# A graph attention layer that streams a 256 MB adjacency matrix: TensorE turns two chunks of the next strip before its maxima, the target rows are computed two pieces later, the index work of narrow strips moves forward, and x is read back into unused parts of the ring

## The reference, cut to what matters

```python
h = jnp.maximum(_layernorm(x, axis=-1), 0.0)                    # x: [8192, 128]
proj = jnp.einsum('nf,hfo->hno', h, W)                          # 4 heads
scores = jax.nn.leaky_relu(s_src[:, :, None] + s_tgt[:, None, :], negative_slope=0.2)
attn = jax.nn.softmax(mask[None, :, :] + scores, axis=1)        # mask: adj, [8192, 8192], values up to 1e9
vals = jnp.einsum('hij,hjo->hio', attn, proj)
vals = jax.nn.elu(vals + h[None, :, :])
out = x + vals.mean(axis=0)
```

## Time and profile before

| what | value |
|---|---|
| median of 3 runs | 993.73 us (992.29 to 1092.76) |
| the profiled execution | 993.13 us, span 991.4 us |
| busy share of the span | DVE 81%, PE 74%, ACT 69%, POOL 24% |
| mean DMA rate over the span | 297 GB/s (290.27 MB by SP's queue, 4.20 MB by POOL's) |
| exponentials, L498 | 512 of 1086 ns, and 512 readings of the sum of 196 ns |
| chunks turned, L440 | 4096 transposes |
| maxima of wide pieces, L557 and L561 | 3.12 us each on the mean |

### The profile page before, as it was taken

The page is one execution under the profiler, slowest core; times in us unless marked ns, Lnnn a source line. Parts: engine busy times, 40 slices in busy tenths (PEclk is TensorE's granted clock), DMA queues, the critical chain, the costliest instruction groups (busy, mean ns, idle before and its releaser), DMA issues.

```text
span 991.4 us, 14968 instructions
## 1 busy us (share of the span) xinstructions
PE 734.1 (74%) x4995; PEld 609.6 (61%) x4995; DVE 807.4 (81%) x812; ACT 684.3 (69%) x1173; POOL 234.7 (24%) x164
## 2 busy tenths in 40 slices
PE   0419597797797797797797797797797798609882
PEld 0317477777777677677677677687687686504330
DVE  3976888888888888888888888888888877327996
ACT  0598496696696696696786786786786788544542
POOL 1000211221221221221212212212212202215885
PEclk9759798898898898898898898998998999859997
DMA  9999999999999999999999999999999976076111
GB/s 245 337 382 384 372 370 337 370 331 325 369 330 323 370 328 325 369 327 323 372 325 321 373 324 325 373 326 324 375 323 324 364 234 173 9 207 150 53 54 55
DMA packets 224068, 294.93 MB, mean 297 GB/s; under 512 B 4512, under 2 KB 218016, under 8 KB 224032
## 3 DMA queue, kind: packets, MB, share of 16 engines
q1 hardware_dynamic: 214816, 290.27, 85.7%
q0 software_dynamic: 9216, 4.20, 3.5%
HBM read 281.80 MB, written 12.65 MB: 297 GB/s over the span
## 4 chain that ended last, share of the span: by engine, by line
PE 33%; DVE 28%; issue 11%; ACT 10%; DMA 8%; POOL 6%; SPq 2%; ACTq 0%; POOLq 0%; DVEq 0%
PE ps L440 23%; DVE arena L561 19%; ACT ps L498 9%; PE ps L405 7%; DMA arena<-in_adj 6%; POOL arena L391 4%; DVE arena L570 3%; SPq L332 2%; DVE arena L578 2%; POOL arena L395 2%; DMA sums<-arena 2%; PE ps L424 1%; DVE arena L623 1%; ACT arena L519 1%; PE ps L412 1%
## 5 line engine op out<-in xcount | busy, mean ns | idle before, releaser
L498 ACT ACTIVATE ps<-ps,arena 128x1024 f32<-128x1024 f32 x512 | 556.0, 1086 | 225.6 <-PE ps L440 198.8
L440 PE MATMUL ps<-ident,arena 128*128 128x128 f32 x4096 | 572.3, 289 | 52.1 <-ACT ps L498 50.1
L440 PEld LDWEIGHTS ps<-ident,arena 128*128 128x128 f32 x4096 | 480.1, 149 | 130.3 <-ACT ps L498 126.3
L561 DVE TENSOR_TENSOR arena<-arena 128x3072 f32<-128x3072 f32 (+2 forms) x115 | 359.3, 3125 | 13.6 <-DMA arena<-in_adj 10.3
L378 POOL DMA_INDIRECT sums<-arena x64 | 157.0, 2453 | 641.4 <-DVE arena L617 313.6
L405 PE MATMUL ps<-ident,arena 128*128 128x128 f32 x512 | 93.2, 342 | 152.6 <-DVE arena L570 151.1
L405 PEld LDWEIGHTS ps<-ident,arena 128*128 128x128 f32 x512 | 80.7, 183 | 157.9 <-issue 89.0
L578 DVE TENSOR_REDUCE arena<-ps 128x1 f32<-128x1024 f32 x64 | 78.3, 1224 | 54.2 <-PE ps L405 54.2
L498 ACT ACTIVATION_READ_ACCUMULATOR ps<-ps,arena 128x1 f32 x512 | 100.2, 196 | 0.0
L557 DVE TENSOR_TENSOR arena<-arena 128x3072 f32<-128x3072 f32 (+2 forms) x23 | 71.8, 3122 | 16.4 <-DMA arena<-in_adj 16.4
L583 DVE SCALAR_TENSOR_TENSOR ps<-ps,arena 128x1024 f32<-128x1024 f32 x64 | 82.1, 1283 | 0.3 <-issue 0.3
(11 more groups left out here) (74 smaller groups left out, 195.8 us busy)
## 6 DMA issues: line engine op xcount, KB each, us to landing
arena<-in_adj SPq DMA_DIRECT2D x160, 1536.0 KB, 13.7
arena<-in_adj SPq DMA_DIRECT2D x16, 512.0 KB, 7.2
arena<-in_adj SPq DMA_DIRECT2D x8, 1024.0 KB, 11.0
sums<-arena SPq DMA_DIRECT2D x1, 4160.0 KB, 22.4
arena<-sums SPq DMA_DIRECT2D x8, 512.0 KB, 7.3
out<-arena SPq DMA_DIRECT2D x16, 256.0 KB, 2.3
sums<-arena POOLq DMA_INDIRECT x64, 7.2
w_sb<-in_L_gnn_W SPq DMA_DIRECT2D x1, 256.0 KB, 2.7
```

The costliest lines, as they stand in the source:

```text
L440: mm = pe.transpose(turned_ps[n % 2][:, m, :], piece(i, r, nq)[:, m, q * P:(q + 1) * P], ident[:, :])
L498: act.activation(turned_ps[n % 2], turned_ps[n % 2], ACT.Exp, scale=KAPPA, bias=cert[:, i, q, G:G + 1], accum_out=cert[:, i, q, r:r + 1]). ...
L561: dve.tensor_tensor(acc_of(nq), acc_of(nq), piece(i, r, nq), ALU.max).then_inc(f_acc, 1)
```

## The change

It does five things.

1. PE turns chunks c0 and c1 of a strip before that strip's `turn_maxima` of sub-strip 0: at the end of the strip before it, behind that strip's last chunk (`EARLY = 2`; for strip 0 before the strips begin). Inside a strip `turn_maxima` of sub-strip 1 then follows that of sub-strip 0 directly.
2. DVE computes the target rows after the fifth `piece_max` of the next strip (piece 5), no longer after the third (piece 3).
3. In the strip of 256 columns `turn_idx`, `sum_same` and `copy_sum` stand after chunks 5, 8 and 9 (before: 8, 13, 15), in the last strip of 128 columns after chunks 2, 3 and 4 (before: 5, 7, 7). For wide strips they stay at 8, 13 and 15.
4. x is read into parts of slots 8 to 11 that the last, narrow strip doesn't use (16 row tiles in each), in four DMAs that SP issues directly behind the last piece of adj, without the wait for all chunks.
5. The tail's buffers `e` and `s2` are separate tiles in the front of these four slots. Their sizes and the instructions on them are the same.

```diff
+    LAST_SLOT = 8
+    XT = NT // (RING - LAST_SLOT)
...
-    x_rows = D.take([NT, O])
...
-    e = D.take([2, 2, H, O])
     m = D.take([4, 2, H, O])
-    s2 = D.take([4, 2, 2, O])
     s1 = D.take([4, 2, O])
+    e, s2, x_rows = [], [], []
+    for b in range(RING - LAST_SLOT):
+        X = Arena(c["arena"], S0 + (LAST_SLOT + b) * RT * WIDE)
+        if b < 2:
+            e.append(X.take([2, H, O]))
+        else:
+            s2 += [X.take([2, 2, O]), X.take([2, 2, O])]
+        x_rows.append(X.take([XT, O]))
...
-    IDX_AT, SUM_AT, COPY_AT = 8, 13, 15
+    IDX_AT = {1: 2, 2: 5, 3: 8}
+    SUM_AT = {1: 3, 2: 8, 3: 13}
+    COPY_AT = {1: 4, 2: 9, 3: 15}
+    EARLY = 2
...
-            sp.wait_ge(f_turn, NT * G)
-            for k in range(2):
-                tiles = slice(k * NT // 2, (k + 1) * NT // 2)
-                sp.dma_start(x_rows[:, tiles, :], x_t[:, tiles, :]).then_inc(t_x, 16)
+            for k in range(RING - LAST_SLOT):
+                sp.dma_start(x_rows[k], x_t[:, k * XT:(k + 1) * XT, :]).then_inc(t_x, 16)
...
+            def turn_chunk(g, i, n):
+                nq = subs(g, i)
+                r, q = order(nq)[n]
+                pe.wait_ge(f_exp, at(g, i, n) + 1)
+                if q == 0:
+                    pe.wait_ge(f_in[slot(i, r)], landed(g, i, r))
+                for m in range(RT):
+                    mm = pe.transpose(turned_ps[n % 2][:, m, :], piece(i, r, nq)[:, m, q * P:(q + 1) * P], ident[:, :])
+                mm.then_inc(f_turn, 1)
+
             def strip(g, i):
...
                 turn_maxima(g, i, 0)
-                for n, (r, q) in enumerate(chunks):
+                for n in range(EARLY, nq * G):
                     if n % LEAD == LEAD - 1 and n // LEAD + 1 < nq:
                         turn_maxima(g, i, n // LEAD + 1)
...
+                    turn_chunk(g, i, n)
                     if not first_strip(g, i):
-                        if n == min(IDX_AT, nq * G - 3):
+                        if n == IDX_AT[nq]:
                             turn_idx(*former_of(g, i))
-                        if n == min(SUM_AT, nq * G - 1):
+                        if n == SUM_AT[nq]:
                             sum_same(*former_of(g, i))
+                if not last_strip(g, i):
+                    for n in range(EARLY):
+                        turn_chunk(*latter_of(g, i), n)
...
-                    if not first_strip(g, i) and n == min(COPY_AT, nq * G - 1):
+                    if not first_strip(g, i) and n == COPY_AT[nq]:
                         copy_sum(*former_of(g, i))
...
                     piece_max(*after, 3)
+                    piece_max(*after, 4)
+                    piece_max(*after, 5)
                 if not first_strip(g, i):
                     find_target(*before)
                 if not last_strip(g, i):
-                    piece_max(*after, 4)
-                    piece_max(*after, 5)
                     piece_max(*after, 6)
```

More of the change, by code:

```diff
@@ L167, in peaked_path @@
     stage = D.take([2, QUAD * P])
-    e = D.take([2, 2, H, O])
     m = D.take([4, 2, H, O])
-    s2 = D.take([4, 2, 2, O])
     s1 = D.take([4, 2, O])
-    assert D.at <= S0 + RING * RT * WIDE
+    assert D.at <= S0 + LAST_SLOT * RT * WIDE
+    e, s2, x_rows = [], [], []
[6 more added lines that the diff above has]
+        x_rows.append(X.take([XT, O]))
+        assert X.at <= S0 + (LAST_SLOT + b + 1) * RT * WIDE
     turned_ps = [c["psum"][b][:, :].rearrange("p (t i) -> p t i", i=P) for b in range(2)]
@@ L390, in _ @@
                     pool.wait_ge(t_s1, w - 3)
-                pool.tensor_tensor(s2[:, w % 4], m[:, w % 4, :, 0:2, :], m[:, w % 4, :, 2:4, :], ALU.add).then_inc(t_s2, 1)
+                pool.tensor_tensor(s2[w % 4], m[:, w % 4, :, 0:2, :], m[:, w % 4, :, 2:4, :], ALU.add).then_inc(t_s2, 1)
                 pool.wait_ge(t_s2, w + 1)
@@ L394, in _ @@
                     pool.wait_ge(t_o, w - 3)
-                pool.tensor_tensor(s1[:, w % 4], s2[:, w % 4, :, 0, :], s2[:, w % 4, :, 1, :], ALU.add).then_inc(t_s1, 1)
+                pool.tensor_tensor(s1[:, w % 4], s2[w % 4][:, :, 0, :], s2[w % 4][:, :, 1, :], ALU.add).then_inc(t_s1, 1)
         @block.tensor
@@ L427, in sum_same @@
                 mm.then_inc(f_sum, 1)
+            def turn_chunk(g, i, n):
[7 more added lines that the diff above has]
+                mm.then_inc(f_turn, 1)
             def strip(g, i):
-                nq, Q = subs(g, i), number(g, i)
-                chunks = order(nq)
+                nq = subs(g, i)
                 turn_maxima(g, i, 0)
-                for n, (r, q) in enumerate(chunks):
+                for n in range(EARLY, nq * G):
                     if n % LEAD == LEAD - 1 and n // LEAD + 1 < nq:
                         turn_maxima(g, i, n // LEAD + 1)
[L436 to L441, removed]
+                    turn_chunk(g, i, n)
                     if not first_strip(g, i):
-                        if n == min(IDX_AT, nq * G - 3):
+                        if n == IDX_AT[nq]:
                             turn_idx(*former_of(g, i))
-                        if n == min(SUM_AT, nq * G - 1):
+                        if n == SUM_AT[nq]:
                             sum_same(*former_of(g, i))
+                if not last_strip(g, i):
+                    for n in range(EARLY):
+                        turn_chunk(*latter_of(g, i), n)
             def turn_sums(k):
@@ L467, in _ @@
             pe.wait_ge(s_ident, 1)
+            for n in range(EARLY):
+                turn_chunk(0, 0, n)
             strips_of(pe, strip)
@@ L543, in _ @@
                     act.wait_ge(t_m, w - 1)
-                act.activation(e[:, w % 2], v_ps[w % 3], ACT.Exp, scale=1.0 / PART, bias=e_bias).then_inc(t_e, 1)
+                act.activation(e[w % 2], v_ps[w % 3], ACT.Exp, scale=1.0 / PART, bias=e_bias).then_inc(t_e, 1)
                 k = w * 2 // QUAD + 2
@@ L691, in elu @@
                     dve.wait_ge(t_s2, w - 3)
-                dve.scalar_tensor_tensor(m[:, w % 4], e[:, w % 2], PART, v_ps[w % 3],
+                dve.scalar_tensor_tensor(m[:, w % 4], e[w % 2], PART, v_ps[w % 3],
                                          ALU.min, ALU.max).then_inc(t_m, 1)
@@ L697, in finish @@
                 dve.wait_ge(t_s1, w + 1)
-                dve.scalar_tensor_tensor(osb[:, tiles, :], s1[:, w % 4], -1.0, x_rows[:, tiles, :],
+                dve.scalar_tensor_tensor(osb[:, tiles, :], s1[:, w % 4], -1.0, x_rows[2 * w // XT][:, 2 * w % XT:2 * w % XT + 2, :],
                                          ALU.add, ALU.add).then_inc(t_o, 1)
@@ L741, in _ @@
             assert count[0] == CHECKS
-            dve.wait_ge(t_x, 32)
+            dve.wait_ge(t_x, 16 * (RING - LAST_SLOT))
             for w in range(PAIRS + 4):
```

## The result

| | before | changed |
|---|---|---|
| median | 993.68 us | 937.42 us (935.8 to 938.15) |
| profiled span | 991.4 us | 934.1 us |
| mean granted clock of TensorE | 0.89 | 0.93 |

The ratio is 0.9436, 95% interval 0.9417 to 0.9455. The forecast was 943 in a range of 921 to 966. One of the four executions of the kernel before took 1092.76 us, and the ratio is taken without it.

What follows compares the result with a forecast made beforehand. No engine was full: a ring of waits bound each strip through three loops (DVE, ACT with PE, DMA). Middle strips 39.2 us, then -0.9, 4.2 and 7.8 at the end, gave 50.3 off 993.13: 943 us, range 921 to 966.

Steps and rivals of the forecast that it cites:

- DVE's and PE's loops: Rings of waits in wide strips: DVE's at 34.4 us, ACT and PE's at 34.5, so a 34.5 us period, clock up.
- fallen strips: Wide strips where PE's clock falls: 35.7 us each, expected in two of three, for a mean period of 35.3.
- the hole: PE idle 3.0 us between a strip's first and second turns of maxima, where its clock can fall, costing 1.2 us.
- Strip 20: First strip after the 18 middle periods, 34.38 us before: 0.9 us lost to the clock's risk.
- strip 21: Next-to-last strip, 29.55 us before: PE bounds it at 24.8, saving 4.8, less 0.6 for the clock: 4.2.
- M(22) to the last landing: From strip 22's first turn of maxima to the last add's landing: 7.8 us saved, 2.8 by an earlier first add.
- chunks c0 and c1 ahead: In wide strips PE turns them while idle, nothing added; DVE's last reduction starts 9.4 us into the strip, not 10.8.
- `find_target` two pieces later: In DVE's loop in wide strips: its stop of 1.7 us goes and nothing takes its place, with 5 us to spare.
- A: Rival: PE's clock holds, all middle strips take 34.5 us, 66.1 us less, 927 us; chance 0.25.
- B: Rival: PE's clock falls in each strip and stays down past c3, 36.6 us a strip, 969 us; chance 0.13.
- E: Rival: the DMA queue is full, the period stays at 37.5 us, only the end's 11 us are gained, 982; chance 0.08.
- D: Rival, slower: one more low clock stretch a strip on PE loses 2.6 us, period 39.2, 1016 us; chance 0.04.

Runs made afterwards that it cites:

- E3: The changed kernel with 16 transposes of the identity, whose result nobody reads, between each strip's first and second turn of maxima: 927.67 us, ratio 0.9337.
- E7: The changed kernel with x read, to its new place, only after all chunks are turned: 941.23 us, ratio 0.949.
- E8: The changed kernel with the narrow strips' index work put back at its old places: 941.16 us, ratio 0.9485.
- E1: The kernel before with one edit, `find_target` moved behind the next strip's fifth `piece_max`: 936.42 us, ratio 0.9434.
- E2: The changed kernel with only the two chunks ahead left; `find_target`, narrow strips' index work and x's read time put back: 1001.36 us, ratio 1.0071.
- E6: The changed kernel with no chunk turned ahead (`EARLY = 0`): 926.60 us, ratio 0.9336.
- E4: The changed kernel with one chunk turned ahead, not two (`EARLY = 1`): 930.08 us, ratio 0.9369.
- E11: The changed kernel without look-ahead, with half of each piece not read from strip 3 on, same instructions: 925.3 us, ratio 0.9304.
- E5: The kernel before with 16 transposes of the identity, whose result nobody reads, behind each strip's last chunk: 972.16 us, ratio 0.9796.

## Why the prediction was right, and where it was not

**Right, with the sum near.** 50.3 us were forecast, 56.3 came. In the strips the forecast had 39.2 us, and 45.3 came: DVE's and PE's loops at 34.5 were 34.2 to 34.3, the second turn of maxima stood at M+4.0 (forecast 4.1), fallen strips took 35.2 to 36.0 (35.7), but the clock fell in 7 of 18 and not in 12. At M = 605.01 DVE was ready about 0.2 us before PE, so the loops did meet. That the clock falls over the hole was a mechanism taken from two rows, and E3 confirmed it. The Trainium skill (TensorE: Matmul & The Clock Gate, section on HAM oscillation) would have had it stay up over a gap of this length; here it fell over an idle gap of 2.93 us in 7 middle strips, and the measurement decides. One reading of the rows was off without a term resting on it: the DMA engines stood still for under three microseconds in the strip at M = 377.92 (a share of 0.46 at 389 to 390, 0.02 at 390 to 392, 0.91 at 392 to 393), not for four.

**The end, nearly right with two errors that cancel.** Strip 20 lost nothing (forecast 0.9), strip 21 gained 3.6 (4.2; its 25.95 us lie above the 24.8 to 25.4 that were to be the sign), and M(22) to the last landing gained 7.7 (7.8). In that last term I put strip 21's first add at M+12.0; it came at 819.39, M+14.2, since x stretched two adds of strip 20 (8.00 and 6.26 us), and the third landed at M+13.3, not at M+12. The chain from there took 11.4 us, not 13.5, because adds that nothing disturbs follow each other in 4.1 us, not 5.1. That the two errors are of one size is luck. E7 and E8 show that both moves work in the way described, 4 to 5 us each.

**Wrong: the credit.** The step "chunks c0 and c1 ahead" is where the forecast put the turn at the upper clock and the shorter way to DVE's last reduction, 1.4 us of the 3.0; the step "`find_target` two pieces later" got only its stop of 1.7. E1 shows that the second alone gives both, and E2 that the first alone gives neither. The time came out near all the same, because the sum was worked out for both edits together. What failed in my working is that I held PE's idle time at the strip's end at 4.0 us for the kernel without look-ahead. That time was PE waiting for DVE; with DVE's stop gone it is 2.2 us. The clock then fell in 6 of 18 strips (E1) and in 8 (E6), and there the low stretch cost little: strip lengths of 34.5 to 35.3 us, and a third turn of maxima at M+8.5 to 9.1, where quick strips have M+8.2. c0's exponential then waits for the bias and not for PE (E1), so to have c0 and c1 ready brings nothing. I also costed the look-ahead as free. It isn't: it moves PE's idle time to one place of 2.93 us, where the clock falls in 7 strips, no more than without it, but the low stretch then stands ahead of DVE's last reduction (third turn at M+9.2 to 9.8) and costs 1.0 to 1.8 us (E3 and E4 get 10 and 7 us back), and it puts two instructions that wait for ACT ahead of the turn for which DVE is ready, 6 us in strips 20 and 21 (E6). Without it the rest of the change is worth 66 us.

**The rivals.** A (the clock holds, 927) is what E3 reached with the clock up. E6 reached the same time in another way, with the clock falling in 8 strips and strips 20 and 21 6 us shorter. B (it falls in each strip) is out with 7 of 18. E (the queue is full) is out by E11. D's mechanism, a low stretch that lies in a worse place, is E2's: 0.7% slower, less than D's 1016, since the strip had one low stretch in its new place and not two.

## What to carry to other kernels

An engine's idle time that ends on another engine is not a constant of the schedule: when a stop is taken out of the other's loop, work it out anew before filling it, and see what it does to TensorE's clock. Where a low stretch of the clock lies counts as well as how often it comes: 6 to 8 falls in 18 strips cost up to 1.1 us each at the start of a strip and up to 1.8 us behind the hole. Work moved ahead on an engine that runs in order leaves a hole where it stood and puts its own wait in front of what followed; here both cost, and nothing was gained, because the bias and not the chunk was what came last. When several edits go in together and the sum comes out right, the parts can still be wrong: run each alone and all but each.

## What the runs showed of the hardware that I had not expected

- The granted clock fell over shorter idle times than four microseconds. Where the longest in a strip was 2.06 us it fell in 3 of 18 strips (E4), where it was 2.2 us in 6 (E1) and 8 (E6), at 2.93 us in 7, and with 1.58 and 2.93 us in the same strip in 17 (E2). In three of the seven it fell about 1 us after the hole had ended. 16 transposes whose result nobody reads, put at the end of each strip, made the kernel before 2% faster (E5), and in the hole they made the changed kernel 1% faster (E3).
- A DMA share of 1.08 at 371 GB/s did not mean that the DMA engines set the period: with half of the bytes left out it stayed at 34.2 us (E11).
- With the filled hole PE stopped at two places of the profiled execution, each time for 6.3 and then 3.6 us, with no releaser in the trace (E3); two executions of five were that much longer. What it waited for is open.
